# Attention with a mixture of experts: first row tiles shared otherwise between engines, one tile's transposes put behind the values before it, and four smaller moves

## The reference, cut to what matters

```
x: (4, 1024, 256), float32;  weights Wq, Wk, Wv, Wo: (256, 256);  8 experts, W1: (8, 256, 1024), W2: (8, 1024, 256)
xn = layernorm(x)
q, k, v = xn Wq' + bq, xn Wk' + bk, xn Wv' + bv
qk = q k'
theta = 0.5 + 0.2 sigmoid(qk) + 0.15 tanh(qk) + 0.1 relu(qk)
s = softmax(theta) v Wo' + bo
e = argmax(xn Wr + br)                                 (one expert for each token)
y = gelu(xn W1[e] + b1[e]) W2[e] + b2[e]
out = x + s * silu(y)
```

## Time and profile before

| | |
|---|---|
| median of 3 runs | 527.48 us (527.33 to 527.98) |
| the profiled execution, its own time | 527.64 us |
| its span in the trace | 525.6 us |
| PE busy | 515.6 us (98%) |
| DVE busy | 402.6 us (77%) |
| ACT busy | 344.6 us (66%) |
| POOL busy | 195.8 us (37%) |
| granted TensorE clock | 1.00 |

### The profile page before, as it was taken

One profiled execution on the slowest core, in us unless ns is written; L12 is line 12 of the kernel. 1 busy time (PEld: TensorE's weight loads), 2 busy tenths in 40 slices (PEclk: granted clock), 3 DMA queues, 4 the chain that ended last, 5 costly groups with the idle time before them and its releaser, 6 DMA issues.

```text
span 525.6 us, 10829 instructions
## 1 busy us (share of the span) xinstructions
PE 515.6 (98%) x3773; PEld 484.3 (92%) x3773; DVE 402.6 (77%) x811; ACT 344.6 (66%) x633; POOL 195.8 (37%) x227
## 2 busy tenths in 40 slices
PE   7999999999999999999999989999999999999997
PEld 6899998899989999899999979998999989999997
DVE  5898689946578855598555688768999998867887
ACT  4789778437356733466343575899787786777884
POOL 3218419913112222222112222005676785342441
PEclk9999999999999999999999999999999999999999
DMA  8964720031635711247311421005233232211221
GB/s 266 344 225 176 285 81 1 2 120 32 230 123 151 255 55 41 61 133 237 112 40 40 136 70 42 21 22 190 62 99 113 71 114 87 62 44 49 60 71 51
DMA packets 40754, 57.49 MB, mean 109 GB/s; under 512 B 3654, under 2 KB 35788, under 8 KB 40156
## 3 DMA queue, kind: packets, MB, share of 16 engines
q1 hardware_dynamic: 35452, 46.02, 26.5%
q0 software_dynamic: 3488, 9.47, 6.4%
q10 hardware_dynamic: 1760, 1.32, 0.8%
HBM read 41.07 MB, written 17.56 MB: 112 GB/s over the span
## 4 chain that ended last, share of the span: by engine, by line
PE 86%; ACT 6%; DVE 5%; issue 1%; POOL 1%; DMA 1%; ACTq 0%; DVEq 0%
PE ps L899 26%; PE ps L901 25%; PE ps L900 25%; PE ps L1014 5%; DVE stats L1375 2%; PE ps L1193 1%; PE ps L1080 1%; ACT hid L763 1%; POOL xn_all L464 1%; DMA xn_all<-in_L_attn_x_dram 1%; PE ps L1070 1%; ACT relu_s L628 1%; ACT tanh_s L625 1%; ACT theta L624 1%; PE ps L1045 1%
## 5 line engine op out<-in xcount | busy, mean ns | idle before, releaser
L899 PE MATMUL ps<-v_hi,pT_hi 128*128 128x258 f32 x256 | 74.9, 293 | 0.2
L747 ACT ACTIVATE hid<-ps,b_now 128x256 f32<-128x256 f32 x128 | 53.7, 472 | 29.7 <-PE ps L901 28.8
L900 PE MATMUL ps<-v_lo,pT_hi 128*128 128x258 f32 x256 | 72.5, 283 | 0.0
L901 PE MATMUL ps<-v_hi,pT_lo 128*128 128x258 f32 x256 | 72.3, 282 | 0.0
L1430 DVE SCALAR_TENSOR_TENSOR theta<-tanh_s,theta 128x512 f32<-128x512 f32 x64 | 47.3, 739 | 23.5 <-ACT tanh_s L625 22.9
L899 PE MATMUL ps<-w_hi_even,hidT_h 128*128 128x256 f32 x200 | 58.5, 293 | 1.6 <-DVE hidT_l L1727 1.1
L636 ACT ACTIVATE theta<-theta,neg_max 128x512 f32<-128x512 f32 x64 | 43.0, 720 | 24.9 <-DVE neg_max L1436 24.6
L519 POOL COPY unit_token<-sorted_token 128x2 int32 x19 | 4.5, 238 | 142.9 <-PE ps L1193 142.9
L901 PE MATMUL ps<-w_hi_even,hidT_l 128*128 128x256 f32 x200 | 56.6, 283 | 0.0
L900 PE MATMUL ps<-w_lo_even,hidT_h 128*128 128x256 f32 x200 | 56.6, 283 | 0.0
L778 ACT ACTIVATE g_sb<-y_sb 128x512 f32<-128x512 f32 x20 | 12.6, 631 | 65.8 <-DVE y_sb L1742 65.8
(11 more groups left out here) (258 smaller groups left out, 1641.5 us busy)
## 6 DMA issues: line engine op xcount, KB each, us to landing
w_raw_odd<-in_L_ffn_W_dram SPq DMA_DIRECT2D x10, 1024.0 KB
w_raw_even<-in_L_ffn_W_dram SPq DMA_DIRECT2D x6, 1024.0 KB
sorted_g<-g_sb SPq DMA_DIRECT2D x20, 256.0 KB, 2.2
xn_rows<-xn_all SPq DMA_DIRECT2D x4, 1024.0 KB, 6.2
x_tile<-in_L_attn_x_dram SPq DMA_DIRECT2D x32, 128.0 KB, 2.2
out_dram<-g_tile SPq DMA_DIRECT2D x32, 128.0 KB, 1.7
xn_all<-in_L_attn_x_dram SPq DMA_DIRECT2D x3, 1024.0 KB, 12.4
kept_xT<-passing_xT SPq DMA_DIRECT2D x2, 1024.0 KB, 4.0
```

The source lines that it names most:

```text
L747: last = nc.scalar.activation(hid[:, j % 2, c * UNIT:(c + 1) * UNIT], ps[:, HID_BANK + j, c * UNIT:(c + 1) * UNIT], ACT.Gelu, bias=b1_now[ ...
L899: mm(dst, a_hi, b_hi, start=first, stop=False)
L900: mm(dst, a_hi, b_lo, start=False, stop=False)
L901: return mm(dst, a_lo, b_hi, start=False, stop=last)
```

## The change

Six edits. ACT normalizes tile 0 alone and DVE tiles 1 and 2. The second `If` of an expert's first unit becomes `Else`, on ACT and on DVE. The four matmuls of G are issued together, and `route_0` of tiles 4 to 7 behind them. At tile 10 (TPB + 2) PE issues `weighted(9)` ahead of `transposes(10)` and `job(10)`, and the explicit wait for `pT_ready` is gone there. On DVE the statistics of tiles 16 and 17 come ahead of `thetas(0, [0])`, those of 18 and 19 behind it, and the later group is shorter by two.

```diff
@@ ACT
-            normalize(range(2))
+            normalize(range(1))
@@ ACT, units_of
-                with act.If(full < u0 + 1):
+                with act.Else():
                     gelus_half(u0, par, beside=lambda: high_w1(w1_landed, other, raw[0], slice(0, 1)))
@@ PE
                     last = mm(ps[:, 7, m * D:(m + 1) * D], wv_raw[:, ec, m * P:(m + 1) * P], woT[:, ec, :],
                               start=ec == 0, stop=ec == DC - 1)
-                    if m == DC - 1 and ec == DC - 1:
-                        last.then_inc(G_done, 1)
-                    route_0(4 + 2 * m + ec)
+            last.then_inc(G_done, 1)
+            for t in range(4, TPB):
+                route_0(t)
@@ PE, batches 1 to 3
+                elif n == TPB + 2:
+                    weighted(n - 1)
+                    transposes(n)
+                    job(n)
                 else:
                     pe.wait_ge(pT_ready, n * 2)
                     transposes(n)
@@ DVE
-            normalize(range(2, 3))
+            normalize(range(1, 3))
@@ DVE
-            thetas(0, [0])
             dve.wait_ge(x_in[2], 16)
             row_statistics(range(2 * TPB, 2 * TPB + 2))
+            thetas(0, [0])
+            row_statistics(range(2 * TPB + 2, 2 * TPB + 4))
             dve.wait_ge(G_high, 1)
@@ DVE
-            row_statistics(range(2 * TPB + 2, 3 * TPB))
+            row_statistics(range(2 * TPB + 4, 3 * TPB))
@@ DVE, first_unit_of
-                with dve.If(full < u0 + 1):
+                with dve.Else():
```

More of the change, by code:

```diff
@@ L1760, in first_unit_of @@
                     low_w1(e, other, 0)
-                with dve.If(full < u + 1):
+                with dve.Else():
                     parts_half(u, beside=lambda: low_w1(e, other, 0))
```

## The result

The changed kernel takes 529.31 us (median of nine executions, 529.01 to 531.41) against 527.58 us before on the same chip. The ratio of the means is 1.0044, with an interval of 1.0031 to 1.0057; that of the medians is 1.0033. It is slower, as forecast, but by 0.3 to 0.4% instead of 0.27%, and it is not one time but two. In five executions the granted clock is 1.000 over the span and the time 529.01 to 529.31 us; in four it is 0.996 or 0.997 and the time 530.35 to 531.41 us. The forecast describes the first kind. The profiled execution, 530.37 us with a span of 528.6 us, is of the second. (In the removed line of DVE's branch, the diff ahead of the prediction names the parameter `u0`; in the code it is `u`.)

The account below looks back on a forecast made before the run. PE, busy 98% of the span, was taken as the bound. Terms 1.45 + 0.1 - 0.13 = +1.4 us took 527.64 to 529.1; with the median 0.16 lower, the forecast was 528.9 us, range 527.9 to 529.7.

Parts of the forecast that it names:

- rival (d): PE's 2.6 us stand at tile 10 drops the clock to half rate, adding 1.9: 530.8 us; chance 0.06.
- The tile 10 order: PE at tile 10: values of tile 9 wait for finish(8) until 361.23, so tile 12's scores start 1.45 us later.
- rival (c): At tile 10 finish(8) is not late, values fill PE's lost time, next scores at 363.9: 526.3 us; chance 0.06.
- First rows and statistics: Kernel head: bias product +0.2 us at 10.3, shorter late statistics worth at most 0.10; net +0.1 us.
- Rival (b): Kernel head: first rows and moved statistics bring POOL 0.40 us forward: 528.4 us; chance 0.13.
- The group behind G: Reordered matmuls of G and the router, ahead of PE's wait at 43.79: cost zero, -0.3 without that cover.
- Else: Seventh expert: ACT's two instructions of line 804 go, -0.13 us; bounds +0.13 at double jump cost, -0.2 with DVE's branch.

Follow-up runs that it names:

- experiment 3: The changed kernel with twenty unused transposes of the identity filling PE's stand before the values of tile 9: 528.98 us, ratio 1.0026.
- experiment 5: The changed kernel with DVE's finish(8) put later, behind the thetas of tile 11, so PE stands longer: 535.29 us, ratio 1.0144.
- experiment 6: The changed kernel with DVE's finish(8) between the transposed parts of tile 9 and low_u, so PE stands shorter: 527.81 us, ratio 1.0006.
- experiment 2: The kernel before with the tile 10 edit alone: 530.34 us, ratio 1.0047.
- experiment 4: The changed kernel with DVE's finish(8) ahead of the second half of tile 10's thetas: 526.81 us, ratio 0.9988.
- experiment 8: The kernel before with the first rows edit alone: 527.90 us, ratio 1.0007.
- experiment 10: The changed kernel without the first rows edit, with finish(8) ahead of the second half of tile 10's thetas: 526.85 us, ratio 0.9984.
- Experiment 7: The changed kernel without first rows and both Else, with finish(8) between the halves of tile 10's thetas: 526.67 us, ratio 0.9981.
- experiment 1: The changed kernel without the tile 10 edit: 527.69 us, ratio 1.0003.
- experiment 9: The kernel before with both Else edits alone: 527.69 us, ratio 0.9999.

## Why the prediction was right or wrong

**The step that failed** is rival (d), "The clock falls", held apart at a chance of 0.06 and left out of the sum. Its mechanism was seen, and even its rule was cited; it happens in about half the executions of the changed kernel (4 of 9, and 4 of 5 with the edit alone). Its reason for so low a chance was that no row of before shows a fall in mid-kernel. But no row of before shows a stand of 2.5 us in mid-kernel either: the longest was 1.1, so the trace could not speak against the fall, and the one stand of that length that it had, the 2.93 us at the start, stood ahead of matmuls at half speed. With the stand filled the fall did not come (experiment 3, 0 of 8), with a longer one it came each time (experiment 5, 4 of 4), and with one of 0.9 us it did not (experiment 6, 0 of 10). Its price was 1.3 us in the changed kernel and, by the medians of the two kinds of execution, 530.54 - 529.18 = 1.36 us, not 1.9. The 3.4 us at the lower level were not all spent on matmuls: of the 3.8 assumed, PE ran through 2.93 (the stretch 361.0 to 364.3), of which half is 1.47. Behind a stand of 2.4 us the clock read 0.50, in 8 of 14 executions: the rule of the Trainium skill ("TensorE: Matmul & The Clock Gate", "HAM oscillation — how this bites in real kernels") was right in kind. So chance and price were mis-sized, and the term was missing from the sum. A forecast of 528.9 in half the cases and 528.9 + 1.4 in the other half would have been the fair reading, with a range up to 530.5.

**The tile 10 order: right in mechanism and in size.** +1.45 was forecast and +1.5 read, with `half_s` as the releaser. The 5.2 us of the forecast is 2.86 + 0.79 + 1.50 + 0.1 = 5.25 rounded down, and 5.27 and 5.29 were measured. Experiments 2, 3, 4 and 6 place it from all sides: alone, with the clock held, with the wait gone (363.99 for the 363.9 of rival (c)), and with the wait at 0.9 us, where it costs nothing.

**First rows and statistics: right within what can be measured.** The transposes at 8.91 for 8.85, the bias product at 10.24 for 10.3, the turn 0.09 late for 0.1, and DVE now waits for ACT's square root, the bound that the forecast gave for the gain of the statistics. Rival (b) fell by that row. What each is worth alone is open: experiment 8 gives the rows +0.38 us, and 4 against 10 by their ratios +0.2 (0.9988 against 0.9984), both inside the scatter. Part of what experiment 8 lost is not in the head at all but the longer stand near 322 us, 0.22 us of PE's time. Experiment 7, with the statistics and the group behind G but not the first rows, has its bias product at 10.15, 0.04 late, and its turn at 43.65, 0.14 early; so 0.18 us is for those two together, up to that place.

**The group behind G** was never run by itself. It is in experiment 1, where five edits sum to nothing, and in 7; that it is worth zero was not shown alone.

**Else: the place was right, the sum wrong by 0.2.** The forecast took the 0.13 to the end "since nothing behind it takes up slack". The gain is there, 0.18 us with DVE's part (the forecast's bound was -0.2 "with DVE's own branch"). But the rule missed that a change of ACT's program can make a new wait elsewhere, which costs 0.25. The net, +0.07, lies within its bound of +0.13 by luck: that bound was for a jump of double cost.

**The sum.** For the executions at full clock it was +1.4, and +1.60 was measured (529.18 against 527.58). By PE's rows of the changed kernel it is made of +0.07 from the head (304.56 for 304.49), -0.18 at the wait for `hid` (307.74 for 307.85, so 0.11 early), +0.26 at 322 us (322.55 for 322.40, so 0.15 late) and 1.5 for the order, in all 1.65.

## What to carry to other kernels

When an order on one engine is changed, look up the order of the engine that frees its buffer: the values first cost 1.5 us with DVE's order left as it was, and won 0.7 to 0.9 us (experiments 4 and 7) when `finish` was moved too. A new stand of TensorE that is longer than any in the trace of before has two prices, its length and the clock, and the second belongs in the sum with a chance taken from the nearest stand of its length, not from its absence. A wait that is shorter than before shows a gain only if the engine did not come later to it: read a gain from positions on both sides. Read the granted clock of every execution, not of the profiled one alone: one median over two kinds of execution hides both.

## What the runs showed of the hardware that was not expected

**The fall is a matter of chance from one execution to the next** at the same stand of 2.4 us: 8 of 14 executions (changed kernel and experiment 2). It began at different places: at the end of the stand in the changed kernel (the clock is 0.95 over 360 to 361 us and 0.50 behind it), some six matmuls behind it in experiment 2, and within the stand, past 363 us, in experiment 5. What decides it isn't in the records.

**The start differs as well**, in the same instructions. PE's eight matmuls of line 910, in the changed kernel and in experiment 9:

```profile
6.25 1.99 PE L910 MATMUL ps<-wk_raw,wq_raw 128*128 128x256 f32 x8
```

```profile
6.50 2.88 PE L910 MATMUL ps<-wk_raw,wq_raw 128*128 128x256 f32 x8
```

In the changed kernel they start 0.22 us apart from 6.57 us on; in experiment 9 they start 0.43 apart until about 8.6, in experiment 1 until 9.04. The granted clock reads 1.00 all the while, so that view does not show this slow start. In experiment 1 it put PE's first transposes of rows at 9.72 us instead of 9.18. Edits worth 0.1 us in the head can't be measured against that.

**An ACT program that is shorter by one instruction or branch** stood 0.3 to 0.4 us longer at one place near 316 us, in nine profiles of nine, and in none of three with the old program. The missing normalization of experiment 8 lies at 8 us, some 308 us ahead of that place.
